# Cross attention: both heads' logits in the two row halves of the array, keys and values through a ring filled by SP

## The reference, cut to what matters

```
q = (text @ Wq.T + bq)   k = (video @ Wk.T + bk)   v = (video @ Wv.T + bv)   # heads of 64
logits  = einsum('avhd,bthd->abhvt', k, q) / sqrt(64)
weights = softmax(logits, axis=3)          # over the 64 frames of each video
attn    = einsum('avhd,abhvt->abhtd', v, weights).mean(over the 128 videos)
return attn @ Wo.T + bo
```

## Time and profile before

| | |
|---|---|
| median of 3 runs | 2643.03 us (2639.49 to 2645.39) |
| the profiled execution | 2661.52 us, span 2659.7 us |
| TensorE, weight loads | 2223.3 us (84%), 1588.4 us (60%) |
| VectorE | 2017.1 us (76%) |
| ScalarE, GpSimd | 1757.2 us (66%), 1522.3 us (57%) |
| select stage / attention loop / output stage | about 0 to 137 / 666 to 2269 / 2269 to 2287 us |
| HBM traffic | 27 GB/s over the span |

### The profile page before, as it was taken

One profiled execution on the slowest core, in us unless ns is written; L12 is line 12 of the kernel. 1 busy time (PEld: TensorE's weight loads), 2 busy tenths in 40 slices (PEclk: granted clock), 3 DMA queues, 4 the chain that ended last, 5 costly groups with the idle time before them and its releaser, 6 DMA issues. The chain is left out here.

```text
span 2659.7 us, 48294 instructions
## 1 busy us (share of the span) xinstructions
PE 2223.3 (84%) x12615; PEld 1588.4 (60%) x12616; DVE 2017.1 (76%) x3304; ACT 1757.2 (66%) x4921; POOL 1522.3 (57%) x1668
## 2 busy tenths in 40 slices
PE   4605688673899999999999999999999999767773
PEld 2304577563566666666666666666666666656663
DVE  5806775304799999999999999999999999565554
ACT  2205321352788888888888888888888888225552
POOL 2241342363577777777777777677677677325552
PEclk9757665796899999999999999999999999769997
DMA  6311103111000000000000000000000000311114
GB/s 217 116 39 48 48 25 95 42 42 46 1 0 0 1 0 0 0 0 0 0 0 0 0 0 0 0 0 0 0 0 0 0 0 0 103 36 36 36 36 113
DMA packets 70362, 71.94 MB, mean 27 GB/s; under 512 B 21376, under 2 KB 55296, under 8 KB 70272
## 3 DMA queue, kind: packets, MB, share of 16 engines
q1 hardware_dynamic: 51696, 49.44, 6.4%
q0 software_dynamic: 8192, 16.87, 2.4%
q10 hardware_dynamic: 10384, 4.66, 0.6%
HBM read 53.07 MB, written 17.87 MB: 27 GB/s over the span
## 5 line engine op out<-in xcount | busy, mean ns | idle before, releaser
L1835 POOL TENSOR_TENSOR attend_weights<-attend_weights,attend_scales 128x512 f32<-128x512 f32 x1024 | 1048.3, 1046 | 477.3 <-DVE attend_scales L1751 477.3
L1729 DVE TENSOR_REDUCE attend_maxima<-attend_psL 128x16 fp32r<-128x1024 f32 x512 | 623.8, 1218 | 88.4 <-PE attend_psL L1651 88.4
L1745 DVE TENSOR_REDUCE attend_sums<-attend_weights 128x16 f32<-128x1024 f32 x512 | 618.6, 1208 | 4.3 <-ACT attend_weights L1781 4.1
L1795 ACT ACTIVATE attend_turned<-attend_psT 128x512 f32<-128x512 f32 x1024 | 557.1, 600 | 9.9 <-PE attend_psT L1670 6.6
L1670 PE MATMUL attend_psT<-consts,attend_weights 128*128 128x128 f32 x4096 | 531.2, 272 | 1.1 <-POOL attend_weights L1835 0.9
L1670 PEld LDWEIGHTS attend_psT<-consts,attend_weights 128*128 128x128 f32 x4096 | 477.0, 140 | 70.9 <-POOL attend_weights L1835 3.0
L1683 PE MATMUL attend_psA<-attend_turned,attend_chunk_values 128*64 128x512 f32 x2048 | 495.9, 605 | 0.8 <-ACT attend_turned L1795 0.8
L1789 ACT ACTIVATE attend_weights<-attend_psL,attend_maxima 128x64 f32<-128x64 f32 x2048 | 448.7, 334 | 51.1 <-DVE attend_maxima L1729 51.1
L1650 PE MATMUL attend_psL<-keys,attend_q_high 128*128 (+1 forms) x1024 | 435.3, 425 | 7.1 <-ACT attend_weights L1789 5.5
L1651 PE MATMUL attend_psL<-keys,attend_q_low 128*128 (+1 forms) x1024 | 404.9, 395 | 0.0
L1781 ACT ACTIVATE attend_weights<-attend_psL 128x512 f32<-128x512 f32 x512 | 315.8, 617 | 0.6 <-PE attend_psL L1660 0.6
(11 more groups left out here) (326 smaller groups left out, 2688.3 us busy)
## 6 DMA issues: line engine op xcount, KB each, us to landing
select_xbuf<-in_x_dram SPq DMA_DIRECT2D x16, 1024.0 KB
select_emb<-L_attn_video_embeds_dram ACTq DMA_DIRECT2D x16, 256.0 KB, 3.0
values_gates<-project_vg SPq DMA_DIRECT2D x8, 512.0 KB, 2.6
retain_vg<-values_gates SPq DMA_DIRECT2D x8, 512.0 KB, 3.5
moe2back_back<-result SPq DMA_DIRECT2D x8, 512.0 KB, 7.3
normed<-moe2route_normed SPq DMA_DIRECT2D x4, 520.0 KB, 8.9
moe_w<-in_L_ffn_W_dram SPq DMA_DIRECT2D x1, 2048.0 KB, 10.8
normed<-moe1route_normed SPq DMA_DIRECT2D x4, 512.0 KB, 5.1
```

What stands on the lines that cost most here:

```text
L1729: dve.tensor_reduce(maxima[:, both, :].rearrange("p j v -> p (j v)"), psL[:, both, :].rearrange("p j (v f) -> p (j v) f", f=FR), X, ALU.ma ...
L1745: dve.tensor_reduce(sums[:, both, :].rearrange("p j v -> p (j v)"), weights[:, both, :].rearrange("p j (v f) -> p (j v) f", f=FR), X, ALU. ...
L1795: act.activation(turned[:, parity, :, j * P:(j + 1) * P], psT[:, j % 2, :].rearrange("p (k q) -> p k q", k=SUB), ACT.Copy).then_inc(turned ...
L1835: pool.tensor_tensor(w, w, scales[:, s, :, None].to_broadcast([P, VC, FR]), ALU.mult).then_inc(normalised, 1)
```

## The change

A step now takes half a batch's queries (256, in two tiles) for both heads, instead of one head's 512. Its four units are j = (head j % 2, tile j // 2). A run is a batch: 32 steps, two for each chunk of keys, 256 steps in all. `FIRST` = 8 steps of a run are written out, the others go by four in a loop.
- Keys: head 0 in partitions 0 to 63, head 1 in 64 to 127; the rounded parts of all keys, then the rests. In the select stage one product, one ScalarE and one VectorE instruction per chunk over 128 partitions replace two each, and `psK` has a second bank for the next chunk. The doubled weights and biases go, with 6 small DMAs and 6 ScalarE copies.
- Logits: 64 rows. For a pair of units (head 0 and head 1 of a tile) three products each, high x high, high x rest, rest x high, alternating between the heads; before, two products of 128 rows per tile. TensorE waits once, for the exponentials of both units.
- Mix: eight products of 256 columns, alternating between the heads' column halves, instead of four of 512.
- Ring: SP copies each chunk's keys (both parts) and values (both heads) from `K.keys` and `K.values` into one of two slots; GpSimd's copy goes, and TensorE waits for the slot every second step.
- Output stage: `stage` and ScalarE's copies go; products of 64 rows read `mixedT` directly, both heads into banks of their own; the loops are written out.

```diff
-                        for h in range(H1):
-                            pe.matmul(psK[:, h, :], wk2[:, h, :], embT[:, s % 2, :], start=True, stop=True).then_inc(keys_ready, 1)
+                        pe.matmul(psK[:, s % 2, :], wkT[:], embT[:, s % 2, :], start=True, stop=True).then_inc(keys_ready, 1)
...
-                        for h in range(H1):
-
-                            dve.wait_ge(key_highs, c * H1 + h + 1)
-                            cols = ds(c * KC + h * KEYS, KC)
-                            dve.scalar_tensor_tensor(K.keys[64:P, cols], psK[64:P, h, :], bk2[64:P, h:h + 1],
-                                                     K.keys[64:P, cols].bitcast(F32), ALU.add, ALU.subtract).then_inc(key_lows, 1)
+
+                        dve.wait_ge(key_highs, c + 1)
+                        dve.scalar_tensor_tensor(K.keys[:, ds(c * KC + KEYS, KC)], psK[:, s % 2, :], bk[:, 0:1],
+                                                 K.keys[:, ds(c * KC, KC)].bitcast(F32), ALU.add, ALU.subtract).then_inc(key_lows, 1)
...
+                    def load(slot, c, uses):
+
+                        if uses is not None:
+                            sp.wait_ge(logits_ready, uses * 8)
+                        sp.dma_start(key_ring[:, slot].bitcast(F32), keys[:, :, ds(c * KC, KC)].bitcast(F32)).then_inc(keys_in[slot], 16)
+                        if uses is not None:
+                            sp.wait_ge(chunks_mixed, uses * 2)
+                        sp.dma_start(value_ring[:, slot].rearrange("p h t e -> p h (t e)"),
+                                     K.values[:, :, ds(c * SUB, SUB), :].rearrange("p h t e -> p h (t e)")).then_inc(values_in[slot], 16)
...
-                    def logits(n, h, key, j):
-
-                        pe.wait_ge(exped, 4 * n + (j + 1))
-                        tile = slice(j * P, (j + 1) * P)
-                        pe.matmul(psL[:, j, :], q_high[h][:, tile], K.keys[:, ds(key, KC)], start=True, stop=False, skip_group_check=True)
-                        pe.matmul(psL[:, j, :], q_low[h][:, tile], K.keys[:, ds(key, KC)], start=False, stop=(SHIFTED_BY[j] != "TensorE"),
-                                  skip_group_check=True).then_inc(logits_ready, 1)
+                    def logits(n, p, k, pair):
+
+                        units = (2 * pair, 2 * pair + 1)
+                        pe.wait_ge(exped, 4 * n + (units[1] + 1))
+                        products = ((q_high, 0), (q_high, 1), (q_low, 0))
+                        for x, (q, part) in enumerate(products):
+                            for j in units:
+                                h, t = unit(j)
+                                tile = slice((k % 2 * 2 + t) * P, (k % 2 * 2 + t + 1) * P)
+                                last = x == len(products) - 1
+                                mm = pe.matmul(psL[:, j, :], q[p][head_rows(h), tile], key_ring[head_rows(h), k // 2, part, :],
+                                               start=(x == 0), stop=(last and SHIFTED_BY[j] != "TensorE"), skip_group_check=True)
+                                if last:
+                                    mm.then_inc(logits_ready, 1)
...
-                        for k in range(SUB):
-                            part = slice((k % 2) * DH1, (k % 2 + 1) * DH1)
-                            mm = pe.matmul(psA[part, :], chunk_values[:, parity, k, :], turned[:, parity, k, :],
-                                           start=(first and k < 2), stop=(k >= SUB - 2), skip_group_check=True)
+                        for t in range(SUB):
+                            for h in range(H1):
+                                mm = pe.matmul(psA[head_rows(h), r * 2 * P:(r + 1) * 2 * P], value_ring[:, slot, h, t, :],
+                                               turned[:, parity, t, h].rearrange("p t l -> p (t l)"),
+                                               start=(first and t == 0), stop=(t == SUB - 1), skip_group_check=True)
```

More of the change, by code:

```diff
@@ L1533, in cross_attention, with head_rows @@
         mixedT = sb("mixedT", [P, B * L])
-        head_sums = (qT, mixedT)
+        def head_rows(h):
+            return slice(h * DH1, (h + 1) * DH1)
+        UNITS = 4
+        STEPS, FIRST, LAG = 2 * NKC, 8, 3
+        SHIFTED_BY = ("ScalarE", "TensorE", "VectorE", "TensorE")
+        shifted_on = {who: [j for j in range(UNITS) if SHIFTED_BY[j] == who] for who in set(SHIFTED_BY)}
+        keys_in = [sem(f"keys_in{s}") for s in range(2)]
+        values_in = [sem(f"values_in{s}") for s in range(2)]
         norm_ready, normT_ready, normT_copied = sem("norm_ready"), sem("normT_ready"), sem("normT_copied")
@@ L1628, in index, with run @@
-            def index(b, h, c):
-                return (b * H1 + h) * NKC + c
+                def run(i, p):
+                    for s in range(FIRST):
+                        step(i, p, s, s % 4, s // 4)
+                    with engine.Fori(0, (STEPS - FIRST) // 4) as it:
+                        for k in range(4):
+                            step(i, p, it * 4 + (FIRST + k), k, it + FIRST // 4)
+                for p in range(2):
+                    run(0, p)
+                with engine.Fori(1, B // 2) as i:
+                    for p in range(2):
+                        run(i, p)
@@ L1632, in exists, with index, quarter @@
+                for s in range(LAG):
+                    step(B // 2, 0, s, s % 4, s // 4)
+            def index(i, p, s):
+                return (i * 2 + p) * STEPS + s
+            def quarter(i, p, q):
+                return (i * 2 + p) * (STEPS // 4) + q
             def exists(n):
-                return not isinstance(n, int) or 0 <= n < CHUNKS
+                return not isinstance(n, int) or 0 <= n < B * STEPS
             def videos(ap):
@@ L1639, in cross_attention, with _ @@
             with nc.Block() as block:
+                @block.sync
+                def _(sp):
+                    keys = K.keys[:].rearrange("p (part n) -> p part n", part=2)
+                    def load(slot, c, uses):
[6 more added lines that the diff above has]
+                                     K.values[:, :, ds(c * SUB, SUB), :].rearrange("p h t e -> p h (t e)")).then_inc(values_in[slot], 16)
+                    for slot in range(2):
+                        load(slot, slot, None)
+                    with sp.Fori(1, NKC // 2) as it:
+                        for slot in range(2):
+                            load(slot, it * 2 + slot, it * 2 + (slot - 1))
+                    with sp.Fori(1, B) as b:
+                        with sp.Fori(0, NKC // 2) as it:
+                            for slot in range(2):
+                                load(slot, it * 2 + slot, b * NKC + it * 2 + (slot - 1))
```

235 lines of the change are left out of this document (94 added, 141 removed).

## The result

The changed kernel takes 2691.17 us in the median (2688.52 to 2694.39, four runs), the kernel before on the same chip 2641.69 (2639.49 to 2645.39, four runs): 1.0186 times as long, with an interval of 1.0169 to 1.0204. The change makes the kernel slower by 49.5 us, where +30 was forecast.

What follows compares the result with a forecast made beforehand. TensorE was taken to bound the attention loop at 6.11 us a step. Terms 64 - 11 - 17 - 3 - 4 + 1 = +30 us on the 2643.0 us median gave 2673 us, range 2528 to 2705.

Steps and rivals of the forecast that it cites:

- (a): Rival, attention loop: the array changes form for nothing and VectorE becomes the bound at 5.81 us; 2532 us; chance 0.18.
- (b): Rival, attention loop: the changes of form cost about half, a step takes 5.85 to 6.1 us; 2545 to 2640; chance 0.10.
- The logits: Attention loop on TensorE: six pairs of 64-row products at 0.23 us replace eight 128-row products, saving 0.48 us a step.
- The four new changes: Attention loop on TensorE: entering and leaving row halves twice a step costs 0.73 us, with ends 0.56 and 0.80.
- Fewer runs: Attention loop: 8 runs fewer, each with a query projection, a rounding and loop turns; -11 us (-6 to -14).
- Select stage: One key rounding a chunk and waits go, less 6 us for VectorE's slower product: -17 us (-10 to -23).
- the parameters' landing: Start of the select stage: six small DMAs fewer before VectorE's last awaited load; -3 us (0 to -4).
- Output stage: Output product: staging copies and their wait go, products run in row halves; -4 us (-1 to -6).
- Ring: SP's key and value copies in the attention loop: nothing in the loop, +1 us at its start.
- (c): Rival, logits: halves of 512 columns don't run together, 1.38 us more a step; 3026 us; chance 0.06.
- (e): Rival, logits: a load cannot pass a matmul of its own row half; +113 us, 2786; chance 0.02.
- (d): Rival, attention loop: the ring's transfers land late, 1.5 us per two steps; +192 us, 2865; chance 0.03.

Runs made afterwards that it cites:

- whole-array version: Changed kernel with its logits as two products of 128 rows per tile instead of three of 64 rows: 2634.50 us, 0.9916 times before.
- the version with them: Changed kernel without row halves (queries projected doubled, four-part key loads) and with all select-stage token products on VectorE: 2578.33 us, 0.9966 times before.

## Why the prediction was right, and where its sizes were off

The direction, the mechanism and the rows that it would show came out: TensorE stays the bound, its queue carries the changes of form, and VectorE's wait before the second maxima grows (0.55 forecast, 0.60 measured). The steady step of 6.405 lies inside the 6.2 to 6.5 that the forecast allowed. That the time lies inside 2528 to 2705 says little, for this range takes in rivals (a) and (b), by which the kernel would be faster. The forecast's own 2640 to 2705 held too, but it does not follow from its terms: with the net at 0 and +84 and the others at their ends it is 2597 to 2711. Nor does the upper end of (b): 6.1 us a step gives 2606, not 2640.

- *The logits*: 6 pairs at 0.23 forecast, 0.231 measured. The saving of 0.48 stands (0.47), and opposite halves do run together.
- *The four new changes*: forecast 0.20 + 0.20 + 0.18 + 0.15 = 0.73. The 0.18 has no row behind it; the prediction itself had read 0.20 before a shift. Measured 0.20 + 0.20 into the row halves, 0.20 before the shift, 0.15 to 0.16 before the transposes: 0.76 by the starts of the instructions. By the whole step against the whole-array version it is 0.77 (0.298 longer, with 0.47 saved at the logits). The net is +0.30 a step and not +0.25, +76 us and not +64. This is 12 of the 19.5 us that were missing; the select stage is 9, and a remainder between the stages' sum and the medians 3, less some 4 that the other terms gave more than forecast.
- *Fewer runs*: the excess over the steady step fell from 22.7 to 10.7 us, -12 for the -11 forecast. A turn of the outer loop costs up to 3.4 us over two steps (7.44 and 8.75) where before's cost 2.0 (6.5 and 7.7), but there are two instead of six. Attend as a whole: +64 for a forecast of 64 - 11 + 1 = +54.
- *Select stage*: in proportion this was mis-sized most, -11.3 for the -20 of its two terms. I allowed 6 us for VectorE's product being slowed by GpSimd's. Its mean went from 3.47 to 4.93 us, 8 x 1.46 = 11.7 us. The earlier trace rows did not hold it, but the two products' rows in the trace of before did: there it started 2.55 to 3.31 us after GpSimd's and always ended 2.15 us after GpSimd's end. From them, starting 2.2 us earlier is worth nothing, because the end stays where it is. Of the parameters' landing I forecast -3; it came at 19.12 instead of 19.89, -0.8.
- *Output stage*: -6.3 for -4, inside its ends.
- *Ring*: nothing in the loop, as forecast; 3.1 + 2.5 us in a row against a margin of 8.5.

The rivals: (a) and (b) fall with the measured 0.77, (c) and (e) with the kernel in one row half, (d) with the ring filled once. That the changes of form cost the time, and not the number of instructions, is shown by the version with one change less: it has the same instructions in another order, and its step is 0.165 shorter. What stays open is why the profiled execution of before was long in retention, and a remainder of 3 us between the stages' sum and the medians. Nor was it tried why the chips' mixture stages differ, or why a turn of the outer loop costs from 1.8 to 5.6 us in the different versions.

## What to carry to other kernels

Packing small products into halves of the array pays for its own slots only if they follow each other long enough: here a visit of three pairs saves 0.24 us and costs 0.36 to 0.40 to enter and leave, so group by form first and count the visits. When one engine's work is moved earlier, look at what its neighbour holds at that moment: a product that starts 2 us earlier beside GpSimd's ended at the same distance behind it. Price the turns of a long loop body and the number of DMAs on a queue from rows as well: here two turns cost 0.47% of the kernel, more than the 0.34% that the version with them had gained, and eight DMAs a batch cost 22 us where their edit was to win 4 to 7.

## What the runs showed of the hardware

- A change of form costs 0.09 to 0.10 us of empty array and the uncovered load behind it (0.06 to 0.11), at the upper clock, and the empty time is the same from column to row halves as from either to the whole array.
- In row halves the two members of a pair start a few nanoseconds apart, and a slot of 512 columns is 0.231 us, hardly less than in the whole array (0.2325).
- A turn of a long outer loop cost TensorE 5.1 to 5.6 us without any semaphore, with a body of two runs of doubled queries; in the changed kernel it was 1.8 and 1.9 us, in its whole-array version 2.7 and 2.8; in before ScalarE stood 2.1 us at each of six turns (12.7 in all) and TensorE 0.9 behind it.
- DMAs from SBUF to SBUF take some 0.63 us of the sync queue each, at 128 as at 512 KB; 128 KB land after 2.3 to 2.4 us, 256 KB after 2.5 and 512 KB after 3.1.
- VectorE's product of two SBUF inputs takes 2.28 us alone; beside one of GpSimd's it ends 2.15 us after that one's end, whether it started 1.09 or 3.31 us behind it.
